# First stage of a state-space and expert kernel: order of table turns, states, evictions and weighing

## The reference, cut to what matters

```python
x_in = x @ in_W.T + in_b
K = exp(dtA[:, :, None] * arange(2048))           # 128 channels, 32 complex modes each
Ceff = Cc * (exp(dtA) - 1.0) / A
k = 2.0 * einsum('hn,hnl->hl', Ceff, K).real
y = irfft(rfft(u, n) * rfft(k, n), n)[..., :2048]  # long convolution per channel
y = gelu(y + u * D_skip[:, None])
# then a gated linear unit, out_W, and the residual; x + layernorm(x) is carried on
```

## Time and profile before

| | us |
|---|---|
| median of 3 runs | 316.31 (316.17 to 316.78) |
| the profiled execution | 317.75 |
| span of its instructions | 316.0 |

### The profile page before, as it was taken

How to read it: one execution, slowest core, us unless ns; L and a number is a source line. 1 busy time by engine, 2 the same in 40 slices (tenths; PEclk the granted TensorE clock), 3 DMA queues, 4 the chain that set the end, 5 groups by cost and what they waited for, 6 DMA issues and landing times.

```text
span 316.0 us, 8652 instructions
## 1 busy us (share of the span) xinstructions
PE 256.7 (81%) x2812; PEld 234.3 (74%) x2812; DVE 230.1 (73%) x842; ACT 163.2 (52%) x318; POOL 165.2 (52%) x218
## 2 busy tenths in 40 slices
PE   1794376584499687999999889998999999999970
PEld 0794366573387455898888779998999999899970
DVE  6999997969952288877778576746868888886251
ACT  0477538459675475666775363534344444444320
POOL 2489400000048002777777777711747777777771
PEclk9999587789789999999999799999999999999995
DMA  5793009669999960111111145343555666664331
GB/s 124 206 389 146 0 23 263 175 173 285 304 308 291 311 203 11 50 52 52 52 59 53 51 125 161 123 130 107 156 150 138 188 166 196 185 193 134 104 84 50
DMA packets 72725, 47.17 MB, mean 149 GB/s; under 512 B 6241, under 2 KB 70129, under 8 KB 72177
## 3 DMA queue, kind: packets, MB, share of 16 engines
q1 hardware_dynamic: 66000, 37.07, 40.0%
q0 software_dynamic: 4096, 8.40, 9.2%
q10 hardware_dynamic: 2592, 1.26, 1.6%
HBM read 28.66 MB, written 18.06 MB: 148 GB/s over the span
## 4 chain that ended last, share of the span: by engine, by line
PE 51%; DVE 17%; issue 9%; DMA 8%; POOL 5%; ACT 4%; DVEq 3%; SPq 2%; POOLq 1%; ACTq 0%
PE bank L1692 9%; PE bank L1703 8%; POOL area L651 5%; PE bank L1608 5%; PE bank L1595 4%; PE bank L1435 3%; PE bank L1497 3%; PE bank L1683 2%; DMA area<-kp_dram 2%; DVE stats L703 2%; DMA kp_dram<-xnT 2%; PE bank L1424 2%; PE bank L1543 2%; PE bank L1535 2%; DVE u L748 2%
## 5 line engine op out<-in xcount | busy, mean ns | idle before, releaser
L632 POOL DMA_INDIRECT xs_dram<-area x64 | 64.2, 1004 | 41.1 <-issue 40.2
L651 POOL DMA_INDIRECT area<-y_dram,u x64 | 67.1, 1048 | 35.1 <-issue 21.6
L1692 PE MATMUL bank<-xn,v 128*128 128x128 f32 x320 | 43.0, 277 | 0.4 <-DVE x_sb L947 0.3
L1013 DVE COPY v<-v 128x512 f32 x84 | 34.3, 450 | 9.5 <-issue 9.2
L1703 PE MATMUL bank<-v,xn 128*128 128x128 f32 x312 | 41.2, 275 | 0.0
L1692 PEld LDWEIGHTS bank<-xn,v 128*128 128x128 f32 x320 | 38.8, 192 | 1.8 <-DVE x_sb L947 0.5
L1703 PEld LDWEIGHTS bank<-v,xn 128*128 128x128 f32 x312 | 38.0, 192 | 0.0
L1360 ACT ACTIVATE xn<-bank 128x512 f32<-128x512 f32 x40 | 23.9, 597 | 21.6 <-PE bank L1692 21.0
L1355 ACT COPY xn<-bank 128x256 f32<-128x256 f32 x41 | 15.2, 372 | 26.4 <-PE bank L1683 26.4
L1072 DVE COPY u<-bank 128x256 f32<-128x256 f32 x39 | 16.4, 420 | 10.3 <-PE bank L1703 10.0
L1092 DVE SCALAR_TENSOR_TENSOR x_sb<-area,u,x_sb 128x128 f32<-128x128 f32 x64 | 18.3, 347 | 4.1 <-DMA area<-y_dram,u 2.7
(11 more groups left out here) (319 smaller groups left out, 603.6 us busy)
## 6 DMA issues: line engine op xcount, KB each, us to landing
area<-kp_dram SPq DMA_DIRECT2D x12, 512.0 KB, 6.6
y_dram<-xinit SPq DMA_DIRECT2D x1, 4992.0 KB, 19.4
area<-xs_dram SPq DMA_DIRECT2D x78, 64.0 KB, 1.9
y_dram<-u SPq DMA_DIRECT2D x39, 128.0 KB
x_sb<-in_L_attn_x SPq DMA_DIRECT2D x4, 512.0 KB, 8.2
area<-ab_dram SPq DMA_DIRECT2D x2, 1024.0 KB, 5.9
xn<-ab_dram SPq DMA_DIRECT2D x2, 1024.0 KB, 11.1
xn<-kp_dram SPq DMA_DIRECT2D x4, 512.0 KB, 6.7
```

What stands on the lines that cost most here:

```text
L632: pool.indirect_dma_start(out=xs_dram.ap(), out_offset=bass.IndirectOffsetOnAxis(ap=pos[:, k, i:i + 1], axis=0), in_=hx[:, i, :], in_offse ...
L651: pool.indirect_dma_start(out=yl[:, k, i, :], out_offset=None, in_=y_dram.ap(), in_offset=bass.IndirectOffsetOnAxis(ap=slot_of[:, k, i:i + ...
L1013: v.tensor_copy(wc[:, z % STEP], v1_flat.rearrange("p (w m) -> p w m", w=2)[:, :, bass.ds(r, HID)]).then_inc(wc_ready, 1)
L1692: last = mm(bank[2 + p % 2][:, HID * j + P * c:HID * j + P * c + P], wc[:, (2 * p + j) % STEP, 1, P * c:P * c + P], xsT[:, p % 3, P * j:P ...
```

## The change

TensorE's order becomes tables, states, impulse for groups 0 to 2, and states, tables, impulse for group 3. ScalarE makes cosine 3 after the eviction of impulse response 1 rather than before, and makes its first 16 `add_norm` tiles after the last impulse response; four of them stood between evictions. VectorE weighs groups 0 and 1 before the products of group 3, and groups 2 and 3 after them. No instruction is added or removed.

```diff
@@ -784,7 +784,6 @@
             v.tensor_scalar(lw[:, 4, :], lw[:, 3, :], -1.0, None, ALU.mult)
             link(v.tensor_scalar(lw[:, 5, :], lw[:, 5, :], -1.0, None, ALU.mult))
             products(2)
-            products(3)
 
             def weigh_states(g):
 
@@ -797,8 +796,11 @@
                 link(v.tensor_tensor(cross, lw[:, 5, x_].unsqueeze(1).unsqueeze(3).broadcast_to(shape), own[:, ::-1], ALU.mult))
                 v.tensor_tensor(st[:, :, x_], st[:, :, x_], cross, ALU.add).then_inc(st_dve, 1)
 
-            for g in range(NG):
-                weigh_states(g)
+            weigh_states(0)
+            weigh_states(1)
+            products(3)
+            weigh_states(2)
+            weigh_states(3)
             dve.wait_ge(st_dve, NG)
             sv = st[:].rearrange("p r x (b j) -> p r x b j", b=B)
             m1, m2 = [rnd[:, 128 * i:128 * i + 128].rearrange("p (r x b) -> p r x b", r=2, x=NX) for i in range(2)]
@@ -1163,11 +1165,17 @@
                 a.activation(mag[:, g].rearrange("p (h n) -> p h n", h=HG), abb[g][:, :, 0:N], ACT.Exp,
                              scale=srow[:, 0:1]).then_inc(mag_ready, 1)
 
-            def sines(g):
+            def sine(g):
                 act.wait_ge(arg_ready, g + 1)
                 a.activation(trig[g][:, 1], trig[g][:, 1], ACT.Sin, scale=TWO_PI)
+
+            def cosine(g):
                 a.activation(trig[g][:, 0], trig[g][:, 0], ACT.Sin, scale=-TWO_PI,
                              bias=halfpi[:]).then_inc(trig_ready, 1)
+
+            def sines(g):
+                sine(g)
+                cosine(g)
 
             for i in range(2):
                 evict_xnT(i)
@@ -1223,16 +1231,15 @@
             evict_k(0)
             sines(2)
             evict_v2(1)
-            sines(3)
+            sine(3)
             evict_k(1)
-            act.wait_ge(scaled, 1)
+            cosine(3)
             evict_v2(2)
-            add_norm(0, 2)
             evict_k(2)
             evict_v2(3)
-            add_norm(2, 4)
             evict_k(3)
-            add_norm(4, 16)
+            act.wait_ge(scaled, 1)
+            add_norm(0, 16)
 
             def copy_states(ks, lo, hi):
                 for k in ks:
@@ -1472,10 +1479,15 @@
             turn_tables(0)
             states(0)
             impulse(0)
-            for g in range(1, NG):
-                states(g)
-                turn_tables(g)
-                impulse(g)
+            turn_tables(1)
+            states(1)
+            impulse(1)
+            turn_tables(2)
+            states(2)
+            impulse(2)
+            states(3)
+            turn_tables(3)
+            impulse(3)
             pe.wait_ge(k_ready, NG)
             pe.wait_ge(v2_act, 16)
             pe.wait_ge(st_dve, NG)
```

## The result

The changed kernel takes 321.36 us (median of four runs, 321.02 to 321.89) against 316.40 us for the kernel before: 1.0109 times as long, with a 95% interval of 1.0062 to 1.0157. The prediction was 315.0 us, faster; the time lies above its range. The profiled execution of after took 321.02 us with a span of 319.3, against 317.75 and 316.0 of before, so the two traces show 3.3 us of the 4.96 between the medians; the profiled execution of before lies above its four timed ones (316.17 to 316.78).

What follows compares the result with a forecast made beforehand. It took the first stage as bound by TensorE with late instruction blocks, then the last store and load, with state copies ending almost together; minus 1.35 us on the slower of two chains gave 315.0 us, range 312.8 to 317.4.

Steps and rivals of the forecast that it cites:

- Where the blocks fall: TensorE's 256-instruction block boundaries: 113, 64, 31 matmuls into states of groups 1, 2, 3; only the last gaps, 0.8 to 2.4 us.
- part on group 1: Group 1, tables before states: last table copy at 51.5, impulse done 53.7 to 54.5, store at about 55.0; gains nothing.
- The third gap: TensorE's wait for an instruction block 31 matmuls into group 3's states: 0.8 to 2.4 us, not there before.
- The upper bound: Latest arrival of the block in group 3's states: 8.85 us after the one before, at 67.35; 62.8 was taken.
- The scan chain: Group 3's states, VectorE's weighing and scan, ScalarE's state copies: minus 1.8 us (minus 1.15 to minus 2.45).
- the k chain: Group 3's impulse response, store, last load: response done at 69.0 against 69.75, store landing about 1.35 us earlier.
- Products 3: VectorE's products of group 3, behind two weighings: run 56.95 to 59.3, costing nothing if TensorE needs them later.
- the cover: Slack between the end of VectorE's group 3 products (59.3) and TensorE reaching group 3's states (60.4): 1.1 us.
- The activations at the end: Four ScalarE input-normalising activations moved behind the last k eviction: 1.6 us more, hidden, with 0.5 us of wait left.
- Slower: the block waits out the load: Rival: group 3's block waits for group 1's loads, TensorE on at about 67.3; 318.9 us, chance 0.21.
- The transfers set the end: Rival: full DMA holds stores behind loads, so group 2's and 3's loads move only 0.4 us; 315.9 us, chance 0.21.
- The block comes in time: Rival: the boundary in group 3's states costs nothing, both chains gain about 4 us; 312.3 us, chance 0.15.

Runs made afterwards that it cites:

- the version without the wait: Changed kernel with two turned tables of groups 1 and 2 in a fourth bank, so TensorE waits for no eviction mid-tables: 316.87 us, 0.9960; repeated 316.06 us, 0.9951.
- the early evictions: Changed kernel with a fourth table bank, ScalarE evicting group 1 ahead of group 2's sines, VectorE as before the change: 317.54 us, 0.9980 to the kernel before.

## Why the prediction was wrong

**The step that failed is "Where the blocks fall".** The places were right (113, 64 and 31 matmuls in; the profile shows 113, no gap, 30). The prices were not. At the first boundary none was set: TensorE "enters the first at 52.35", the moment at which it comes there, as if the block lay ready. By the price of 3.86 us from the boundary at 44.65 it would have, at 48.5, and in the version without the wait it was there at 48.31. What the prediction left out is that a wait early in a block also holds back the next block. It wrote the reverse: "nothing in the new order stops TensorE early in a block as the eviction wait did at 52". The fourth bank's wait does just that, 22 instructions in, and its end, 49.7, stood in the prediction's own part on group 1. From its release (49.34) the block took 6.24 us: a gap of 3.60 us where none was costed. At the second boundary "no gap" held, because TensorE then took 6 us over the block.

**The third gap** was costed at 0.8 to 2.4 us and measured 3.71: the block came 5.5 us after the one before it, not 3.86 to 4.7, because group 1's loads filled the DMA meanwhile (without them it was 3.5). The upper bound, TensorE on at 67.35, nearly met the 67.20 measured, but by another sum: TensorE entered the block before at 61.7 instead of 58.5, and 5.5 us stand where 8.85 were added.

**What follows from these.** Group 1's store left at 58.37 instead of the predicted 55.0. From there group 2 took what was worked out: from the start of its tables to the end of its impulse 57.65 to 63.2, 5.6 us, against 6.0 to 6.8; only it began 3.3 us late. Group 3's states ended at 68.75 instead of 64.05. The scan chain lost 2.9 us instead of gaining 1.8; the k chain, instead of gaining 0.75 to 1.35, lost 3.5 at the store and 2.6 at the last landing (89.27 against 86.64).

**Right, point by point.** Products 3 hid behind TensorE's late arrival: 60.00 to 62.36, against group 3's states from 63.03; the cover was 0.7 us, not 1.1, with everything 3 us later. The activations at the end stayed hidden, with 1.05 us of ScalarE's wait for the scan left. ScalarE's and VectorE's parts together cost nothing in the old order, as costed (1.0017, interval around 1).

**The rivals.** "Slower: the block waits out the load" came nearest, and its numbers meet the trace: TensorE on at 67.20 (it said 67.3), states done at 68.75 (68.5), the first read of the states 2.92 us late (2.6). That is in part luck. It had no gap in group 1's states and let TensorE enter the block before the late one at 58.5 instead of 61.7; and the late block did not wait out the loads, for it came while they still filled the DMA engines. In time it said 318.9, and 321.36 was measured: a loss of 2.0 to 5.0 us by the interval, and 3.3 in the profiled pair. Its chance of 0.21 was too low because 4.7 us after a wait was taken as the upper price, from a row in which the loads had ended within it. "The transfers set the end" is right in that a store that leaves into the loads of the group before is held up. That the end itself hangs on it is not shown: where it came out so, with shifted boundaries in the old order and with the early evictions, a gap in group 3's states opened or grew as well. "The block comes in time" never came about, since even with quiet DMA 1.63 us of the third gap stay. The rule that stood beside it, from the Trainium skill, page "Runtime: NRT & Kernel Launch", section "Instruction fetch mechanics" (a crossing is "mostly hidden"), does not hold here: crossings in the first stage showed gaps of up to 4.62 us.

**Open.** Why the timed runs of the changed kernel with 64 empty instructions stay above those of before, though in its trace the states are read as early; at which instruction between 62 and 86 the next block is asked for, since the request itself does not show; and how much of the 1.7 us by which the medians differ more than the traces is more than the spread between runs.

## What to carry to other kernels

Count instructions from one "issue" gap to the next and see where a reordering puts the boundaries, and above all which waits come to stand in the first third of a block: such a wait delays the next block as well, and if transfers fill the DMA engines meanwhile, the block took 5 to 6 us here instead of 3.5 to 4. A gap that is moved is not removed: look which boundary and which load come to lie on each other next, and take the wait away (here one more bank) rather than shift it. A store that leaves earlier gains little when the loads of another queue hold it up.

## What the runs showed of the hardware

- The time from one block of 256 instructions to the next, where TensorE wanted it sooner, was 3.5 to 4.1 us with the DMA engines at a share of up to 0.60 in that time (3.86 at 0.16; 4.11 at 0.12 in the old order shifted by 64; 3.84 at 0.55 and 3.8 at 0.60 with the fourth bank; 3.5 with no loads, counted from the end of a wait), and 5.1 to 6.2 us where Hankel loads kept them busier (5.1 at 0.84, 5.5 at 1.09, 5.8 at 1.06; 6.24 at 0.96, this one from the end of a wait).
- After a wait 22, 38 or 62 instructions into a block the next block came 5.9 to 6.2 us after the wait's end, with a gap of 3.2 to 3.6 us; after one at 86 there was no gap.
- The time from a store's issue to its loads' issue went from 2.3 to 5.1 and 5.8 us when it left into the loads of the group before.
